# Disentangled attention: the context-to-position term by stationary query rows and on-chip transfers

## What is computed

```python
def _L0_attn_b_ref(hidden_states, ...):        # H = 16 heads, hd = 8 features each
    q, k, v = shape_heads(...), shape_heads(...), shape_heads(...)
    scores = jnp.einsum('bhsd,bhkd->bhsk', q, k) / jnp.sqrt(hd * 3)
    re = layernorm(rel_emb)                    # 64 rows of relative positions
    pos_k, pos_q = shape_heads(re @ Wpk + bpk), shape_heads(re @ Wpq + bpq)
    rel = _rel_pos(S)                          # bucket of s - k, so it depends on s - k alone
    c2p = jnp.einsum('bhsd,hkd->bhsk', q, pos_k)
    c2p = take_along_axis(c2p, clip(rel + 32, 0, 63), axis=-1)
    p2c = jnp.einsum('bhsd,hkd->bhsk', k, pos_q)
    p2c = take_along_axis(p2c, clip(-rel + 32, 0, 63), axis=-1)
    scores = scores + c2p / sqrt(2 * hd) + swapaxes(p2c) / sqrt(2 * hd)
    ctx = einsum('bhsk,bhkd->bhsd', softmax(scores), v)
    return ctx @ Wo + bo
```

## Time and profile before

| | us |
|---|---|
| median of 3 runs (lowest to highest) | 1324.26 (1322.44 to 1327.71) |
| the profiled execution, its own time | 1330.51 |
| its span, first to last instruction | 1328.7 |
| first fill of `attend` on PE, at | 414.89 |
| first z of the first half on DVE (line 1460), at | 438.87 |
| one half in the loop (from a pair fill at 610.89 to the same at 632.10) | 21.2 |
| last `back` of the last half on PE, at | 1121.54 |

### The profile page before, as it was taken

How to read it: one execution, slowest core, us unless ns; L and a number is a source line. 1 busy time by engine, 2 the same in 40 slices (tenths; PEclk the granted TensorE clock), 3 DMA queues, 4 the chain that set the end, 5 groups by cost and what they waited for, 6 DMA issues and landing times. The chain is left out here.

```text
span 1328.7 us, 34742 instructions
## 1 busy us (share of the span) xinstructions
PE 1048.3 (79%) x9380; PEld 834.1 (63%) x9380; DVE 863.0 (65%) x2997; ACT 727.5 (55%) x1755; POOL 460.4 (35%) x506
## 2 busy tenths in 40 slices
PE   4793515787353899999999999999999998734886
PEld 3793513777232677777777777777777776624776
DVE  6886754555570677777777777777677775652554
ACT  2236411344282677777777777777677774212443
POOL 2503213765200433333333333333333332005764
PEclk9897556999585899999999999999999998656999
DMA  5920052331263222221212222221312220033431
GB/s 136 227 52 0 0 180 92 111 103 54 72 254 120 64 59 62 59 68 50 69 50 69 56 63 67 59 69 50 69 50 69 55 55 1 1 147 97 114 96 42
DMA packets 83508, 103.23 MB, mean 78 GB/s; under 512 B 16473, under 2 KB 71200, under 8 KB 82944
## 3 DMA queue, kind: packets, MB, share of 16 engines
q1 hardware_dynamic: 77824, 89.92, 25.1%
q0 software_dynamic: 5632, 12.70, 2.8%
HBM read 67.86 MB, written 35.74 MB: 78 GB/s over the span
## 5 line engine op out<-in xcount | busy, mean ns | idle before, releaser
L1230 POOL TENSOR_SCALAR ds_scores<-ds_scores,ds_max 128x256 f32<-128x256 f32 x256 | 236.3, 923 | 434.3 <-DVE ds_max L1468 434.2
L1460 DVE TENSOR_TENSOR ds_p2c<-ds_bank,ds_p2c 128x512 f32<-128x512 f32 x256 | 176.4, 689 | 147.9 <-PE ds_bank L1289 113.4
L1468 DVE CUSTOM_DVE_ANT_0 ds_scores<-ds_bank,ds_p2c 128x256 f32<-128x256 f32 x512 | 197.2, 423 | 0.2 <-DVE ds_p2c L1460 0.2
L1289 PE MATMUL ds_bank<-all_constants,ds_c2p_t 128*128 128x128 f32 x1024 | 165.4, 284 | 0.0
L1407 ACT ACTIVATE all_xt<-ds_bank 128x512 f32<-128x512 f32 x256 | 152.6, 596 | 21.4 <-PE ds_bank L1307 8.9
L1307 PE MATMUL ds_bank<-all_constants,ds_scores 128*128 128x128 f32 x1024 | 154.6, 273 | 2.4 <-ACT all_xt L1407 1.6
L1289 PEld LDWEIGHTS ds_bank<-all_constants,ds_c2p_t 128*128 128x128 f32 x1024 | 111.3, 141 | 31.9 <-issue 20.7
L1307 PEld LDWEIGHTS ds_bank<-all_constants,ds_scores 128*128 128x128 f32 x1024 | 120.2, 140 | 7.6 <-issue 2.0
L1390 ACT ACTIVATE ds_c2p_t<-ds_bank 128x256 f32<-128x256 f32 x256 | 77.6, 390 | 56.7 <-PE ds_bank L1280 56.7
L1383 ACT ACTIVATE ds_p2c<-ds_bank 64x512 f32<-64x512 f32 x128 | 75.7, 591 | 54.7 <-PE ds_bank L1261 31.6
L1280 PE MATMUL ds_bank<-d_qr,ds_tab 64*128 64x128 f32 x1024 | 77.3, 292 | 33.1 <-DMA ds_tab<-scratch_tables 27.8
(11 more groups left out here) (285 smaller groups left out, 2011.8 us busy)
## 6 DMA issues: line engine op xcount, KB each, us to landing
ds_tab<-scratch_tables SPq DMA_DIRECT2D x64, 248.0 KB, 3.5
slots_in<-all_zero SPq DMA_DIRECT2D x2, 5180.0 KB, 37.9
ds_qs<-scratch_q_parts SPq DMA_DIRECT2D x32, 288.0 KB
ds_ks<-scratch_k_parts SPq DMA_DIRECT2D x96, 96.0 KB
d_qr<-scratch_qk SPq DMA_DIRECT2D x512, 4.0 KB
d_kr<-scratch_qk SPq DMA_DIRECT2D x512, 4.0 KB
0fe_xb<-slots_in SPq DMA_DIRECT2D x40, 129.5 KB, 2.1
1fe_xb<-slots_in SPq DMA_DIRECT2D x40, 129.5 KB, 2.1
```

The source lines that it names most:

```text
L1230: pool.tensor_scalar(S[b % NS][:, 1, :], S[b % NS][:, 1, :], mx[:, 2 * b + 1:2 * b + 2], None, ALU.subtract).then_inc(s_sub1, 1)
L1289: last = pe.transpose(pt1[b % 2][:, st * SEQ + kt * P:st * SEQ + (kt + 1) * P], CT[half][:, kt, b, st * P:(st + 1) * P], con["ident"])
L1460: dve.tensor_tensor(z, pt1[b % 2][:, :].rearrange("p (a k) -> p a k", a=2), z, ALU.add).then_inc(s_z, 1)
L1468: last = dve.tensor_tensor_reduce(out=S[b % NS][:, st, :], in0=pqk[b % 2][:, st * SEQ:(st + 1) * SEQ], in1=PC[half][:, st, b, :], scale=1. ...
```

## The change

- The c2p term is computed with the roles turned: the query rows (64 rows by 64 queries) are stationary, and 256 columns of the table move. This gives c2p with queries on partitions, but 64 queries of one position residue of all eight sequences at a time. There are four such fills for a half ("c2p", line 1292 after: 8 fp32 matmuls of 256 columns in 64x64 tiles, into the two banks that t1 had).
- ACT copies the two banks of such a fill into STAGE, a buffer of four slots (1411 after). SP then moves each slot by transfers inside SBUF to the queries' rows, into CT, which now has queries on partitions (`spread`: two transfers of 64 rows to 8 partitions, 1217 after, and one of 128 rows to 16 partitions, 1221 after; 2 KB pieces, 128 KB in each of the two, 256 KB in the third). That makes 12 transfers and 2 MB a half. The copy of fill i+2 waits until the transfers of fill i have landed, since they share slots.
- Gone are t1, the c2p pairs, near, far and edge with their copies, the ENDS of c2p, the four tiles S (scores now stay in PC) and DVE's wait for t2.
- z adds two SBUF tiles (1499 after). DVE waits at the start of a half until all transfers of CT have landed.
- The shift is done by POOL for both halves of the rows (two instructions a step, 1262 after).
- Query and key rows are loaded together: 16 transfers of 8x2x128 for a half instead of 32 of 8x128 (1199 after). SP's order in a half is: wait for scores, five parts, wait for the last fills, two tables, then four times (four row transfers of the next head, the three transfers of a spread). At the start SP issues tables, rows, parts and four spreads of the first half before the rows of the second.
- The order of fills and SHARE are new; `back` stands ahead of the step's fill; a half's first fill waits for all 16 row transfers.

```diff
@@ attend: tiles and order @@
-        CT = [m.sb(f"c2p_t{i}", [P, 2, HALF, SEQ]) for i in range(2)]
+        CT = [m.sb(f"c2p{i}", [P, HALF, 2, SEQ]) for i in range(2)]
+        STAGE = m.sb("stage", [P, 4, 2 * SEQ])
-        S = [m.sb(f"scores{i}", [P, 2, SEQ]) for i in range(NS)]
-        pb, pt1, pqk, pt2, pav = bank[0:2], bank[2:4], bank[4:6], bank[6], bank[7]
+        pb, pc, pqk, pt2, pav = bank[0:2], bank[2:4], bank[4:6], bank[6], bank[7]
-        FILLS = [PAIRS[0][0], PAIRS[0][1], PAIRS[1][0], FARS[0][0], EDGE[0], FARS[0][1], NEAR[0],
-                 PAIRS[1][1], FARS[1][0], NEAR[1], FARS[1][1], EDGE[1]]
+        FILLS = [CROSS[0], CROSS[1], NEAR, CROSS[2], FARS[0], PAIRS[0], CROSS[3], PAIRS[1], FARS[1], EDGE]
-        SHARE = [1, 1, 1, 2, 2, 1, 2, 2]
+        SHARE = [1, 1, 1, 1, 2, 1, 2, 1]
@@ SP @@
+            def load_rows(head, half, first, count):
+                for s in range(first, first + count):
+                    at = slice(s * P, (s + 1) * P)
+                    sp.dma_start(QKR[half][(15 - s) * DB:(16 - s) * DB, :, at],
+                                 dram["qk"][:, bass.ds(head * DB, DB), half * HT + at.start:half * HT + at.stop].rearrange("j p n -> p j n")).then_inc(s_rows[half], 16)
+            def spread(head, half, i):
+                u = 2 * head + half
+                sp.wait_ge(s_cc, CC * u + 2 * i + 1)
+                sp.sem_inc(s_go_sp, 1)
+                for r in range(2):
+                    at = 16 * (2 * i) + 8 * (1 - r)
+                    sp.dma_start(CT[half][at:at + 8, :, :, :].rearrange("p b t k -> p (b t k)"), STAGE[64 * r:64 * (r + 1), 2 * (i % 2), :]).then_inc(s_ct[i % 2], 16)
+                sp.wait_ge(s_cc, CC * u + 2 * i + 2)
+                sp.sem_inc(s_go_sp, 1)
+                at = 16 * (2 * i + 1)
+                sp.dma_start(CT[half][at:at + 16, :, :, :].rearrange("p b t k -> p (b t k)"), STAGE[:, 2 * (i % 2) + 1, :]).then_inc(s_ct[i % 2], 16)
@@ POOL @@
-                        pool.tensor_scalar(S[b % NS][:, 1, :], S[b % NS][:, 1, :], mx[:, 2 * b + 1:2 * b + 2], None,
-                                           ALU.subtract).then_inc(s_sub1, 1)
+                        for st, s_sub in enumerate((s_sub0, s_sub1)):
+                            pool.tensor_scalar(PC[half][:, st, b, :], PC[half][:, st, b, :], mx[:, 2 * b + st:2 * b + st + 1], None,
+                                               ALU.subtract).then_inc(s_sub, 1)
@@ PE: the c2p fill @@
+                    for st in range(2):
+                        for swap in range(2):
+                            g = 8 * st + 2 * where + swap
+                            c = TABLE - SEQ - 16 * g
+                            for tile in range(2):
+                                rows, to = slice(tile * 64, (tile + 1) * 64), tile ^ swap
+                                own = QKR[half][rows, 0, :].rearrange("p (m g) -> p g m", g=NB16)[:, g, 64 * (1 - tile):64 * (2 - tile)]
+                                last = pe.matmul(pc[swap][to * 64:(to + 1) * 64, st * SEQ:(st + 1) * SEQ], own, TAB[half][rows, 0, c:c + SEQ],
+                                                 start=True, stop=True)
@@ ACT @@
+                if what == "c2p":
+                    if where > 1 or not (isinstance(u, int) and u == 0):
+                        act.wait_ge(s_ct[where % 2], CD * u + 48 * (where // 2))
+                    for swap in range(2):
+                        act.wait_ge(s_cm, CM * u + 4 * where + 4)
+                        act.activation(STAGE[:, 2 * (where % 2) + swap, :], pc[swap][:, :], ACT.Copy).then_inc(s_cc, 1)
@@ DVE @@
-                dve.wait_ge(s_t1, step + 1)
                 z = PC[half][:, :, b, :]
-                dve.tensor_tensor(z, pt1[b % 2][:, :].rearrange("p (a k) -> p a k", a=2), z, ALU.add).then_inc(s_z, 1)
-                if before:
-                    shift(*before)
+                dve.tensor_tensor(z, CT[half][:, b, :, :], z, ALU.add).then_inc(s_z, 1)
```

More of the change, by code:

```diff
@@ L1212, in heads @@
                         sp.sem_inc(s_go_sp, 1)
-                        load_rows(head + 1, half)
-            load_rows(0, 0)
+                        sp.wait_ge(s_cm, CM * (u + 1))
+                        sp.sem_inc(s_go_sp, 1)
+                        load_tables(head + 1, half)
+                    for i in range(len(CROSS)):
+                        if not last:
+                            load_rows(head + 1, half, 4 * i, 4)
+                        if not (last and half == 1):
+                            spread(*following(head, half), i)
+            load_tables(0, 0)
+            load_rows(0, 0, 0, 16)
             load_parts(0, 0)
-            load_rows(0, 1)
+            for i in range(len(CROSS)):
+                spread(0, 0, i)
+            load_tables(0, 1)
+            load_rows(0, 1, 0, 16)
             sp.dma_start(bo[:, :], w["bo"].partition_broadcast(P)).then_inc(s_bo, 16)
@@ L1242, in fill @@
                 what, kind, where = FILLS[n]
+                u = 2 * head + half
                 if n == 0:
+                    pe.wait_ge(s_rows[half], 256 * (head + 1))
                     pe.wait_ge(s_tab[half], 32 * (head + 1))
@@ L1257, in fill @@
                 if what == "edge":
-                    pe.wait_ge(s_stack[half], 16 * 6 * (head + 1))
+                    pe.wait_ge(s_stack[half], 16 * 5 * (head + 1))
                     for side, grp, _ in INNER:
                         own = slice(side * 64, (side + 1) * 64)
-                        last = pe.matmul(pb[FIRST[n] % 2][own, :], ENDS[half][:, kind, side * FAR + own.start:side * FAR + own.stop],
-                                         (QS, KS)[kind][half][:, :].rearrange("p (b s) -> p b s", b=HALF)[:, :, grp * 16:grp * 16 + 64],
+                        last = pe.matmul(pb[FIRST[n] % 2][own, :], ENDS[half][:, side * FAR + own.start:side * FAR + own.stop],
+                                         KS[half][:, :].rearrange("p (b s) -> p b s", b=HALF)[:, :, grp * 16:grp * 16 + 64],
                                          start=True, stop=True)
@@ L1283, in fill @@
                             last.then_inc(s_bm, 1)
-            def t1(step, half, b):
-                pe.wait_ge(s_z, step + 1)
-                for st in range(2):
-                    for kt in range(2):
-                        last = pe.transpose(pt1[b % 2][:, st * SEQ + kt * P:st * SEQ + (kt + 1) * P],
-                                            CT[half][:, kt, b, st * P:(st + 1) * P], con["ident"])
-                last.then_inc(s_t1, 1)
             def qk(step, half, b):
@@ L1341, in heads @@
                             av(*before)
+                        if n % 4 == 0 and (before := group_before(head, half, n, 8)):
+                            back(*before)
                         if not (last and half == 1):
@@ L1345, in heads @@
                                 done += 1
-                        if n % 4 == 0 and (before := group_before(head, half, n, 8)):
-                            back(*before)
             pe.sem_inc(s_t2, NS)
@@ L1439, in copy @@
                 what, kind, where = FILLS[n]
-                if what == "far" and kind == 1:
+                if what == "far":
                     side, quad = where
                     dve.wait_ge(s_bm, (2 * head + half) * BM + FIRST[n] + 1)
-                    dve.tensor_copy((CT, PC)[kind][half][:, side, :, quad * 64:(quad + 1) * 64],
+                    dve.tensor_copy(PC[half][:, side, :, quad * 64:(quad + 1) * 64],
                                     pb[FIRST[n] % 2][:, :].rearrange("p (b s) -> p b s", b=HALF)).then_inc(s_bd, 1)
@@ L1471, in scores @@
                 last.then_inc(s_sc, 1)
-            def shift(head, half, b):
-                dve.wait_ge(s_sc, number(head, half, b) + 3)
-                dve.tensor_scalar(S[b % NS][:, 0, :], S[b % NS][:, 0, :], mx[:, 2 * b:2 * b + 1], None, ALU.subtract).then_inc(s_sub0, 1)
             def heads(head, last):
```

112 lines of the change are left out of this document (54 added, 58 removed).

## The result

| | before | after |
|---|---|---|
| median, lowest to highest (us) | 1325.99 (1322.44 to 1328.38, 4 runs) | 1695.55 (1681.54 to 1701.01, 4 runs) |
| ratio of after to before | | 1.277, 95% interval 1.269 to 1.286 |
| span of the profiled execution | 1328.7 | 1699.0 |
| first z of the first half | 438.87 | 446.06 |
| first z of the last half | 1101.93 | 1471.27 |

The change costs 370 us, and the table says where: 7 at the start, 31 x 11.7 = 362 in the halves, 2 at the end. The cause is in the loop.

A forecast was written before the change was run, and what follows sets the result against it. PE bound a half (21.2 us), SP right behind. Afterwards transfers would: 31.8 + 5 = 37 us; 31 x (37 - 21.3) = +487, +14 start, +4 end, giving 1829 us; range 1345 to 2020.

The forecast's parts named there:

- The sign and the cause: Whole kernel: slower, chance 0.82, because transfers inside SBUF to few partitions are slow and set the half.
- case A: Halves of `attend`: the transfers set a half at 37 us; 1829 us, between 1610 and 2020; chance 0.64.
- rival B: Halves of `attend`: quick transfers, SP's 23.3 us of issues bind; 1398 us, between 1350 and 1545; chance 0.18.
- The size of a transfer: Spreads into CT: 2.65 us each at 6.2 GB/s for a partition; 12 make 31.8 us a half.
- The estimate by the Trainium skill: Spreads into CT, by SBUF ports reached: 2.4 to 2.5 us a transfer, a half 35, the whole 1770.
- The loads on the same engines add 5 us: DMA engines in a half: the other loads, 0.24 of 21.3 us, add 5.1 us to the spreads.
- The transfers stay fed: Order in a half: one fill's three transfers (8 us) are always under way while the next is copied; no added waits.
- Start and end: Outside the 31 periods: first z later by 14 us, the last half longer by 4 us.
- PE: PE in a half: 8.1 us go, four c2p fills of 1.0 come; 17.2 us, a lower clock at no cost.
- Two signs: Signs in `attend`: DVE waiting over 10 us for CT before a half's first z; PE busy under 20 us a half.
- Rival C: Halves of `attend`: transfers of about 0.7 us, SP needing 18 us; faster, about 1227 us; chance 0.14.
- POOL and DVE: z beside POOL's shifts: they can lock each other out, at worst 20 us a half; put at no cost.

The follow-up runs named there:

- Wide: The changed kernel, each spread transfer writing as many rows as it reads (64 or 128 rows of 2 KB); 1445.6 us, ratio 1.090.
- afto: The changed kernel with the first spread of a half moved ahead of the tables and first four row transfers in SP's queue; ratio 1.204.
- thino: The changed kernel moving only 256 bytes of each 2 KB piece, first spread issued ahead of tables and first four rows; 1404 us, ratio 1.041.
- dve0: The changed kernel with the shift of the first 128 rows done by DVE again, the second by POOL; 1686.9 us, ratio 1.270.
- thin8od: The changed kernel with 256 bytes per piece, 8 transfers a half (ACT swapping halves), first spread early, DVE doing the first shift; ratio 1.098.
- bpool: The kernel before, with POOL doing both shifts of a step and DVE none; ratio 1.001.

## Why the prediction was right, and where it was off

- **The sign and the cause** were right: transfers into 8 and 16 partitions, at a rate that falls with their number, are the main part. Wide shows it: 250 of 369 us. The time, 1695.55, lies 133 us below the forecast and in the lower part of the range that case A had for itself, 1610 to 2020. The whole range, from 1345, would have held rival B too, so the traces decide for A and not the time.
- **The size of a transfer** was too large: 2.65 us from KS's 6.2 GB/s for a partition; a spread of three took 6.7 us, 2.2 a transfer. 26.8 us a half in place of 31.8, which is 155 us over 31 halves. The estimate by the Trainium skill, 2.4 to 2.5 us a transfer ("SBUF — State Buffer", section "Door 1: The DMA port swizzle (why `[64,N]` ≈ `[32,N]`)"), lay nearer, and so did its total of 1770.
- **"The loads on the same engines add 5 us"** failed: afto has 29.5 us with 26.8 of spreads, so at most 2.7 of the loads are added. The rows of KS are three loads to different sets of 24 partitions, which moved no more than 148 GB/s together; they spoke of narrow transfers beside narrow ones, and not of wide loads beside narrow ones.
- **"The transfers stay fed"** failed. I had looked at PE's order (fills at steps 0 and 1) and not at SP's, where the first spread stands behind parts, tables and four rows. It costs 3.4 us a half (afto). The two failures nearly cancel, 2.3 us too much against 3.4 left out, and that is luck: 26.8 + 2.7 + 3.4 = 32.9 measured, against 31.8 + 5 = 37.
- **Start and end**: +7 in place of +14, for the same too long transfers (4 x 6.7 us from 416 on, and a landing, make 446); +2 in place of +4.
- **PE** was right: a c2p fill costs 1.1 us at full clock (824.23 to 825.33; 1.0 taken), and PE is busy under 19 us a half there (18.6 in thino). In after its clock fell to a mean of 0.81, and it was busy 0.64 of the time, 21 us a half. The slower matmuls do stand in the chain (the fill at 838.73 took 1.84 us, and the staging copy waited for it), which the forecast took as no cost; no run here gives the price.
- **Two signs** came out smaller than named: DVE's wait ahead of its first z was 5.6 us in the mean (172 in 31), not over 10, since the other part of the stall came through ACT's staging copies; and PE's busy time was 21 us, not under 20.
- **Rival B** was right in its own terms: 23.3 us of issues against the 22.9 of thino. A spread issue cost 0.63 us (two in 1.30) and 0.58; I had 0.65. It doesn't bind in after, where the queue has holes.
- **Rival C** is refuted further than by its rate: with the bytes nearly gone and the order mended the half is 22.9 us, longer than before. Its 18 us took SP's issues at the low end of 0.35, the price of a small row load.
- **POOL and DVE**: no cost, as taken (dve0, thin8od, bpool). That the two hold each other up fits the rows: z takes 0.77 us in the mean in place of 0.69, and 5.49 (from 455.22) beside POOL's add of 8.16 (from 452.01). That it stays small because the other waits leave room is my reading, not shown.

## What to carry over

Before results are moved to fewer partitions by transfers, divide the bytes for each destination partition by its rate, here 16 KB at 6 to 8 GB/s, a little over 2 us for each transfer, to 8 partitions as to 16: that sum over a period was nearly a floor here (26.8 us; the shortest half of afto was 26.4). Then follow every landing to the next issue on all queues, the issuing engine's above all: one line's place in SP's order was worth 6% here. And a queue that is as full as the bound is a second bound, even if it was seen idle in an unrolled stretch.
